# A transformer block in float32 on TensorE: the order of reciprocals and key work in the first sequence, and transposing transfers of a quarter of a head each

## The reference

```python
# mask: for each sequence, 5120 of 512*512 products are set to 1, the rest to 0
adj = emb_s * emb_t * softmax(x) * (1 / sqrt(512));  adj[diagonal] = -inf
x = x + (adj is among the 5120 largest)
# block, 16 heads of 128
x1 = ln(x) * (1 + scale1) + shift1
q, k, v = split(x1 @ qkv_w + qkv_b)
attn = softmax(q @ k.T * 128 ** -0.5)
x = x + gate1 * ((attn @ v) @ out_w + out_b)
x2 = ln(x) * (1 + scale2) + shift2
x = x + gate2 * (gelu(x2 @ ffn_w1 + ffn_b1) @ ffn_w2 + ffn_b2)
```

## Time and profile before

| | us |
|---|---|
| median of 3 runs | 1552.96 |
| lowest and highest run | 1552.26, 1553.39 |
| the profiled execution | 1553.78 |
| its span, first to last instruction | 1551.9 |
| TensorE (PE) busy | 1500.0 (97%) |
| VectorE (DVE) busy | 1117.5 (72%) |
| ScalarE (ACT) busy | 885.0 (57%) |
| GpSimd (POOL) busy | 408.0 (26%) |

### The profile page before, as it was taken

One profiled execution on the slowest core, in us unless ns is written; L12 is line 12 of the kernel. 1 busy time (PEld: TensorE's weight loads), 2 busy tenths in 40 slices (PEclk: granted clock), 3 DMA queues, 4 the chain that ended last, 5 costly groups with the idle time before them and its releaser, 6 DMA issues.

```text
span 1551.9 us, 21298 instructions
## 1 busy us (share of the span) xinstructions
PE 1500.0 (97%) x7157; PEld 1245.9 (80%) x7157; DVE 1117.5 (72%) x2424; ACT 885.0 (57%) x1631; POOL 408.0 (26%) x243
## 2 busy tenths in 40 slices
PE   1999899999999999999999999999999999999998
PEld 1877788778888888888878888888878888888987
DVE  7878888876796887776785887776786666664431
ACT  4556677764855666662753666763572655654340
POOL 6713545554120322220000322221000122222000
PEclk9999999999999999999999999999999999999999
DMA  7866799987666677775464877687464786786463
GB/s 292 303 260 188 223 214 270 246 230 283 244 239 233 168 211 202 202 203 190 166 227 184 231 187 211 154 211 217 163 231 181 199 217 152 202 207 161 183 237 119
DMA packets 334508, 327.58 MB, mean 211 GB/s; under 512 B 270752, under 2 KB 275008, under 8 KB 331328
## 3 DMA queue, kind: packets, MB, share of 16 engines
q1 hardware_dynamic: 334112, 325.90, 69.9%
q10 hardware_dynamic: 288, 0.33, 0.1%
HBM read 204.54 MB, written 54.54 MB: 167 GB/s over the span
## 4 chain that ended last, share of the span: by engine, by line
PE 88%; DVE 6%; ACT 2%; DVEq 2%; issue 1%; DMA 1%; SPq 0%; ACTq 0%
PE bank L1390 27%; PE bank L1392 26%; PE bank L1391 26%; PE bank L1712 2%; PE bank L1610 1%; PE bank L1605 1%; DVEq L1216 1%; PE bank L1606 1%; DVE tb L1029 1%; PE bank L1422 1%; ACT halves L892 1%; DVE halves L1233 1%; PE bank L1444 1%; PE bank L1441 1%; PE bank L1440 1%
## 5 line engine op out<-in xcount | busy, mean ns | idle before, releaser
L742 POOL CAST probT<-turned 128x2048 fp32r<-128x2048 f16 x128 | 243.3, 1914 | 699.2 <-DMA turned<-halves 399.6
L1390 PE MATMUL bank<-xT,w 128*128 128x512 f32 x704 | 279.7, 397 | 0.0
L1391 PE MATMUL bank<-xT,w 128*128 128x512 f32 x704 | 273.9, 389 | 0.0
L1392 PE MATMUL bank<-xT,w 128*128 128x512 f32 x704 | 273.8, 389 | 0.0
L885 ACT ACTIVATE prob<-bank,nbias 128x512 f32<-128x512 f32 x256 | 176.4, 690 | 113.1 <-DVE nbias L1217 104.1
L1233 DVE SCALAR_TENSOR_TENSOR halves<-prob,rinv,halves 128x512 f16<-128x512 f32 x256 | 175.4, 748 | 25.7 <-ACT halves L892 25.0
L892 ACT ACTIVATE halves<-prob,rinv 128x512 f16<-128x512 f32 x256 | 164.5, 713 | 32.9 <-DVE rinv L1229 32.9
L1215 DVE TENSOR_REDUCE rowmax<-bank 128x1 f32<-128x512 f32 x256 | 174.4, 681 | 0.3 <-issue 0.3
L1392 PEld LDWEIGHTS bank<-xT,w 128*128 128x128 f32 x704 | 132.1, 188 | 28.0
L1390 PEld LDWEIGHTS bank<-xT,w 128*128 128x128 f32 x704 | 132.9, 189 | 25.0
L1391 PEld LDWEIGHTS bank<-xT,w 128*128 128x128 f32 x704 | 132.4, 188 | 24.9
(11 more groups left out here) (171 smaller groups left out, 3328.8 us busy)
## 6 DMA issues: line engine op xcount, KB each, us to landing
w<-split_weights SPq DMA_DIRECT2D x154, 1024.0 KB, 5.8
split_weights<-w SPq DMA_DIRECT2D x38, 1024.0 KB, 6.6
wraw<-weights_in SPq DMA_DIRECT2D x48, 512.0 KB, 4.8
split_weights<-xT SPq DMA_DIRECT2D x7, 1024.0 KB, 7.6
adaw<-ada_w_in SPq DMA_DIRECT2D x4, 1536.0 KB, 13.1
xr<-x_in SPq DMA_DIRECT2D x4, 1024.0 KB, 6.3
split_weights<-qk SPq DMA_DIRECT2D x3, 1024.0 KB, 7.7
adj<-x_in SPq DMA_DIRECT2D x3, 1024.0 KB, 9.2
```

What stands on the lines that cost most here:

```text
L742: nc.gpsimd.tensor_copy(probT[:, :, :, rows].rearrange("p a j (i t) -> p i (a j) t", i=2), turned_of(h)[:, 2 * pair:2 * pair + 2, :, :]).t ...
L1390: pe.matmul(dst, w_hi_ap, x_hi_ap, start=first, stop=False)
L1391: pe.matmul(dst, w_hi_ap, x_lo_ap, start=False, stop=False)
L1392: return pe.matmul(dst, w_lo_ap, x_hi_ap, start=False, stop=last)
```

## The change

1. In heads 1 to 4 of the first sequence the mask's step of the next sequence stands after the two reciprocals instead of ahead of them, and still ahead of the subtractions.
2. The scaling of the factors (`scur`) leaves the row maxima of head 0 and becomes a step of its own at the start of head 1's work. The reciprocal of the exponential's sums is written into `factor` in place, no longer into `rinv`, which the heads use.
3. In every head of every sequence the two transposing transfers of 128 x 2048 become four of 128 x 1024, each with a semaphore of its own and each issued after its own tile's subtraction; the two casts on POOL become four of half the size, and the counts that others wait for are raised to match.

```diff
-        turned_in, widened = [sem("turned_in0"), sem("turned_in1")], sem("widened")
+        turned_in, widened = [sem(f"turned_in{i}") for i in range(NT)], sem("widened")
...
-                for pair in range(PAIRS):
+                for i in range(NT):
                     if k:
-                        wait_apart(sp, widened, (k - 1) * PAIRS + pair + 1)
-                    wait_apart(sp, p16_lo, k * NT + 2 * (pair + 1))
-                    sp.dma_start_transpose(
-                        turned_of(h)[:, 2 * pair:2 * pair + 2, :, :].rearrange("p i n t -> p (i n) t"),
-                        halves_of(h)[:, 2 * pair:2 * pair + 2, :, :].rearrange("p i a s -> p (i a s)"))\
-                        .then_inc(turned_in[pair], 16)
+                        wait_apart(sp, widened, (k - 1) * NT + i + 1)
+                    wait_apart(sp, p16_lo, k * NT + i + 1)
+                    sp.dma_start_transpose(turned_of(h)[:, i, :, :],
+                                           halves_of(h)[:, i, :, :].rearrange("p a s -> p (a s)"))\
+                        .then_inc(turned_in[i], 16)
...
-                for pair in range(PAIRS):
-                    wait_apart(pool, turned_in[pair], 16 * (k + 1))
+                for i in range(NT):
+                    wait_apart(pool, turned_in[i], 16 * (k + 1))
                     pool.wait_ge(pv_done, b * H + h)
-                    rows = slice(2 * pair * P, 2 * (pair + 1) * P)
                     nc.gpsimd.tensor_copy(
-                        probT[:, :, :, rows].rearrange("p a j (i t) -> p i (a j) t", i=2),
-                        turned_of(h)[:, 2 * pair:2 * pair + 2, :, :]).then_inc(widened, 1)
+                        probT[:, :, :, i * P:(i + 1) * P].rearrange("p a j t -> p (a j) t"),
+                        turned_of(h)[:, i, :, :]).then_inc(widened, 1)
...
-                dve.wait_ge(small_in, 16)
+
+            def scale_s(t):
                 src = small[:, COLS["s"][0]:COLS["s"][1]].rearrange("p (b i) -> p b i", b=B)
                 V.tensor_scalar(scur[:, :], src[:, t, :], float(np.float32(T ** -0.5)), None, ALU.mult)
...
-                V.reciprocal(rinv[:, lo:hi], nxsum[:, lo:hi])
-                dve.drain()
-                V.tensor_tensor(factor[:, lo:hi], rinv[:, lo:hi], scur[:, lo:hi], ALU.mult)
+                V.reciprocal(factor[:, lo:hi], nxsum[:, lo:hi])
+                dve.drain()
+                V.tensor_tensor(factor[:, lo:hi], factor[:, lo:hi], scur[:, lo:hi], ALU.mult)
...
-                keys_first = is_first(b) and 0 < h < FIRST_TOTAL
-                if keys_first:
-                    topk_under_head(b + 1, h)
                 for pair in range(PAIRS):
...
+                keys_first = is_first(b) and 0 < h < FIRST_TOTAL
+                if keys_first:
+                    topk_under_head(b + 1, h)
                 dve.drain()
```

More of the change, by code:

```diff
@@ L887, in head @@
                 if k:
-                    for pair in range(PAIRS):
-                        act_e.wait_ge(turned_in[pair], 16 * k)
+                    for i in range(NT):
+                        act_e.wait_ge(turned_in[i], 16 * k)
                 for i in range(NT):
@@ L1198, in topk_under_head @@
                 elif h == 1:
+                    scale_s(t)
                     topk_adj(t, 0, 2)
@@ L1362, in _ @@
             topk_rowmax(0)
+            dve.wait_ge(small_in, 16)
+            scale_s(0)
             topk_adj(0, 0, 2)
@@ L1532, in attend @@
                     pe.wait_ge(cand_ready, (b + 1) * (STEPS + 1) + (step + 2))
-                pe.wait_ge(widened, (b * H + h + 1) * PAIRS)
+                pe.wait_ge(widened, (b * H + h + 1) * NT)
                 for j in range(NT):
```

## The result

The changed kernel takes 1557.5 us (median of 6 runs, 1557.07 to 1558.67) beside 1552.58 us (6 runs, 1550.46 to 1553.39) for the kernel before. The ratio is 1.0035, 95% interval 1.0022 to 1.0048: it is slower by 4.9 us. The prediction had said 4.6 us faster, 1548.4 with a range of 1546.5 to 1551.8. Sign and range were wrong.

The account below looks back on a forecast made before the run. TensorE was taken as the bound, busy throughout from 395 us, with 8.4 us at most to win in the first sequence. Heads 1 to 4 give 2.9 us and head 13 1.7: 1552.96 - 4.6 = 1548.4 us, range 1546.5 to 1551.8.

Parts of the forecast that it names:

- Heads 2 and 3: First sequence: moved keys no longer meet GpSimd's casts; head 2 takes 14.2 us, head 3 13.7 without its stall.
- from there to S3 4.16: Head 2: 4.16 us from the end of the reciprocals' part to the start of head 3's scores, kept unchanged.
- Head 4, where the new order costs: First sequence: VectorE waits for the exponentials, keys follow; head 4 grows from 16.52 to 16.7 us.
- The scaling of the factors: Moved from head 0, it lets head 1's row maxima start 1.64 us earlier, closing the stall ahead of head 2.
- Head 13: Shorter GpSimd casts block its row sums less; head 14 starts at 315.8 instead of 317.54, 1.7 us won.
- the rule on two inputs: Head 13: two-input VectorE subtractions wait for GpSimd's fourth cast, until 312.0; the gain is 1.3 us instead of 1.7.
- The four transfers on SP: Each half-size transfer holds the queue 1.1 us; the queue is free 0.3 us earlier.
- rival 2: Fixed part in each transfer issue: a quarter holds the queue 1.36 us; 1.5 us gain remains, 1551.5; chance 0.11.
- rival 3: Each transfer issue keeps 2.18 us whatever its size; later loads come late, 25 us against 4.6, so 1574; chance 0.08.

Follow-up runs that it names:

- Experiment 4: Changed kernel plus one wait: in heads 1 to 4 GpSimd forms the rests only behind its head's subtractions; 1551.48 us, ratio 0.9996.
- Experiment 6: Experiment 4's kernel, but in head 4 the keys and first count stand ahead of the reciprocals again; 1547.2 us, ratio 0.9969.
- experiment 7: Changed kernel, but in head 4 the keys and first count stand ahead of the reciprocals again; 1552.29 us, ratio 0.9999.
- Experiment 3: Kernel before, with only the scaling of the factors moved to head 1; 1550.66 us, ratio 0.9991.
- Experiment 8: Kernel before, with the scaling moved and four transfers and casts, reciprocals still behind the keys; 1549.96 us, ratio 0.9984.
- experiment 2: Kernel before, with only the four transfers and casts per head; 1550.33 us, ratio 0.9997.
- experiment 1: Changed kernel with the two large transfers and casts of before, keeping the new order and scaling; 1558.95 us, ratio 1.0048.

## Why the prediction was wrong

**The step that failed** is "Heads 2 and 3". It asked whom the moved keys would meet and found that they no longer meet GpSimd, which is right: in heads 3 and 4 they take 0.41 to 0.69 us, in head 2 0.66 and 0.94 at most, where the trace before has 2.02 and 2.23. It did not ask who else would move. The reciprocals release ScalarE, ScalarE's rounding releases GpSimd's forming of the rests, and that instruction went under the four subtractions, which the sum carried at their old length inside "from there to S3 4.16" and again in head 4's 4.16. For head 1 the sum counted the scaling alone and left the new order out, though it holds there too. The timeline of GpSimd before showed it at 146.59, 0.1 us behind the rounding and 1.2 us behind the last subtraction, so a release 3.6 us earlier had to put it on top of them. The collision was even in the text, with the rule of the Trainium skill ("SBUF — State Buffer", Who interferes with whom), but for head 13 alone. Worked out for heads 1 to 4 by lengths, 2.4 us in each, it comes to more than the 4.6 us of forecast gain, even less the 1 us that heads 1 and 3 had to spare, and would have turned the sign. With that rule the runs agree, also where GpSimd's instruction has one input only: 2.14, 2.14, 2.15 and 2.09 us beside the forming of a rest, 0.78 beside a copy. Experiment 4 confirms the step from the other side: with the rests out of the way S1 to S5 is 58.64, 0.4 from the 58.2 predicted. Part of that closeness is luck, since head 2 is 0.4 us shorter than its forecast and heads 1 and 4 are 0.2 and 0.6 longer.

**A term that the sum did not have** is the clock. The prediction took TensorE's own time as fixed. Head 5, in which TensorE then has no idle piece, lost 1.59 us behind one of 3.99 us, and 2.66 behind one of 3.13 in experiment 4; experiments 6 and 7 shorten the piece and head 5 is at 13.85 and 13.87 again. The Trainium skill ("TensorE: Matmul & The Clock Gate", Part 1) says that idleness halves the clock and activity releases it; the rows agree for these pieces, and show no fall behind the 2.22 us of experiment 7.

**Head 4, where the new order costs**: right in kind. VectorE waited for the exponentials, 2.44 us instead of the 3 predicted, and the keys came behind, at 185.80:

```profile
184.14 1.13 DVE L1224 TENSOR_SCALAR rowsum<-rowsum 128x2 f32<-128x2 f32 x1 [2.44 <-ACT prob L883]
```

The head takes 17.85 us instead of 16.7. Its own collision adds 2.09; head 3's collision delays S4 but not the load, which was issued 0.13 us after S4 and not 1.2, and that takes about 1 back. Experiment 4, without either collision, issues the load 1.54 us after S4, VectorE waits 3.61 us, and the head takes 17.26: the forecast was 0.6 too low. It had set the new order at little more than the 1.48 us wait for weights that goes. Experiment 6 shows what it costs: 2.3 us in head 4 and 2.6 behind it, 4.3 us of the medians.

**The scaling of the factors**: right. Experiment 3 has head 1 at 13.60, the 13.6 of the prediction. In the changed kernel it can't be seen, because head 1 lost more to the collision.

**Head 13**: near in size, 1.47 us (13.35 instead of 14.82) against 1.7, and between that and the 1.3 of the rule on two inputs; but that is partly luck, since another wait came in. The row sums are released as predicted, the second takes 0.83 us. The subtractions then wait 1.40 us for ScalarE, whose high parts wait 1.97 us for the last transfer of head 12:

```profile
313.32 0.83 DVE L1224 TENSOR_SCALAR rowsum<-rowsum 128x2 f32<-128x2 f32 x1
...
315.79 2.84 DVE L1233 SCALAR_TENSOR_TENSOR halves<-prob,rinv,halves 128x512 f16<-128x512 f32 x4 [1.40 <-ACT halves L890]
```
```profile
315.03 2.56 ACT L890 ACTIVATE halves<-prob,rinv 128x512 f16<-128x512 f32 x4 [1.97 <-DMA turned<-halves]
```

Head 12's block on SyncE's queue, before and after:

```profile
300.07 8.22 SPq L537 DMA_TRANSPOSE turned<-halves  x2
```
```profile
303.38 9.61 SPq L537 DMA_TRANSPOSE turned<-halves  x4
```

Counted from S12 the block starts 0.6 us earlier, as predicted, but the four take 1.39 us longer than the two did, so it ends 0.8 later where the prediction had it 0.3 earlier. In the trace of the kernel before ScalarE never waits for a transfer here. Experiment 8 has the same wait (2.07 us on ScalarE) and 13.61 us for this head, experiment 2 has it not, and 13.18. Beside the fourth cast the subtractions took 0.10 us more.

**The four transfers on SP**: a quarter holds the queue for 1.25 us, not 1.1 and not rival 2's 1.36; the block in head 3 takes 5.55 us (1.4 an issue with what lies between), where the two took 4.98 in that place. The end of the block is what counts for head 3's load, and it was not late; in head 12 it was, as above. The 631 cycles that rival 2 takes from the Trainium skill ("DMA: Bandwidth & Descriptors", Why a DMA increments its semaphore by 16 and not by 1) are stated there for transposes from HBM (the chip's main memory) into SBUF (the memory that the engines read). The transfers here go from SBUF to SBUF, and the fixed part that their two lengths give is an estimated 0.3 us, not 0.53. From 395 to 1500 us TensorE is busy 1104.12 of 1105 us, against the earlier trace rows, so rival 3 has no trace here.

From 4.6 us faster to 4.9 us slower is 9.5 us (9.1 between the times, since the forecast started from a median of 1552.96 and the comparison from 1552.58): 6.9 in heads 1 to 4 (65.08 against 58.2), 1.6 in head 5, 0.2 in head 13; the remaining 0.8 has no place that I can name.

## What to carry over

When an edit releases an engine earlier, follow the release through every engine behind it and lay what lands on the critical engine's busiest stretch beside that stretch; that an instruction is moved out of a collision says nothing of what is moved in. A stall of TensorE as long as those behind which the clock fell here, 2.21 us and more, is to be priced with the head behind it. Work that fills a wait is free only where the wait is: one order for all heads was wrong here, since heads 1 to 3 had no wait to fill and head 4 had.

## What the runs showed of the hardware

- Of VectorE's subtractions with two operands in SBUF, the one that starts while GpSimd's instruction is at work waits, and it ends about 0.55 us after that instruction: 2.88 us instead of 0.74 beside the forming of a rest, 1.53 beside a copy. One that is under way when GpSimd's starts is not lengthened (0.74 us in head 3 of experiment 1, with GpSimd 0.07 us behind it). The four together lose 2.09 to 2.15 us beside a forming of a rest and 0.78 beside a copy.
- GpSimd's own instruction loses less: 2.40 to 2.75 us where a subtraction waited for it, 2.94 in that head 3, against 2.41 alone.
- TensorE's clock fell to 1.2 GHz behind idle pieces of 3.13, 3.67, 3.99 and 5.21 us, and cost the next head 2.7, 2.5, 1.6 and 1.4 us; the longer pieces did not cost more. Behind 2.21 us it fell in two kernels, behind 2.22 and 2.01 in another it did not, and behind 1.78 or less no head showed a fall. Why the same length goes either way was not tried. The Trainium skill ("TensorE: Matmul & The Clock Gate", Part 1) says of the rise to full speed under load that its moment varies from run to run; no run here shows whether that is the reason.
- A transposing transfer of 128 x 1024 in float16 holds SyncE's queue for 1.25 us at the median (1.23 to 3.45) and lands in 3.3; one of 128 x 2048 holds it for 2.18. An estimate from these two is a fixed part of some 0.3 us (2 x 1.25 less 2.18).
